# Two attention layers over 128 graphs: own orders for the first and last iterations, VectorE's loop written out, and the values of a layer's four graphs issued together

## The reference

```python
# layer 0
q, k, v = x@Wq+bq, x@Wk+bk, x@Wv+bv
h = softmax(where(adj == 0, -inf, q@k.T / sqrt(32))) @ v      # per head
y = layernorm(h@Wo+bo + x) * gamma + beta
# layer 1, on y
n = layernorm(y)*ln1_g+ln1_b;  q, k, v = n@wq+bq, n@wk+bk, n@wv+bv
o = softmax(q@k.T / sqrt(32) + where(adj > 0, 0.1*adj*adj, -inf)) @ v
x1 = y + o@wo+bo
out = x1 + gelu((layernorm(x1)*ln2_g+ln2_b)@w1+b1)@w2+b2      # w1 is 256x1024
```

## Time and profile before

| | |
|---|---|
| median of 3 runs | 2095.86 us (2091.73 to 2095.98) |
| profiled execution, own time | 2092.55 us |
| its span, first to last instruction | 2090.8 us |
| PE busy | 2040.8 us, 98% |
| ACT, DVE, POOL busy | 1649.2, 1598.8, 1007.9 us |
| mean granted TensorE clock | 0.993 of full |

### The profile page before, as it was taken

One profiled execution on the slowest core, in us unless ns is written; L12 is line 12 of the kernel. 1 busy time (PEld: TensorE's weight loads), 2 busy tenths in 40 slices (PEclk: granted clock), 3 DMA queues, 4 the chain that ended last, 5 costly groups with the idle time before them and its releaser, 6 DMA issues.

```text
span 2090.8 us, 59938 instructions
## 1 busy us (share of the span) xinstructions
PE 2040.8 (98%) x20032; PEld 1828.9 (87%) x20032; DVE 1598.8 (76%) x6911; ACT 1649.2 (79%) x5512; POOL 1007.9 (48%) x780
## 2 busy tenths in 40 slices
PE   6899999999999999999999999999999999999997
PEld 5689989889998889998889988889998889998886
DVE  5887877787877788777778777778777778777863
ACT  4688788878788878788888888887878887878863
POOL 3555445545445545445445445445455455455431
PEclk9999999999999999999999999999999999999999
DMA  4111100111100111100111100111100111101000
GB/s 139 32 32 42 42 27 16 40 40 40 40 18 22 40 40 40 40 11 29 40 40 40 40 10 30 40 40 40 40 10 30 40 40 40 37 13 31 27 11 21
DMA packets 80768, 72.80 MB, mean 35 GB/s; under 512 B 3009, under 2 KB 72257, under 8 KB 80705
## 3 DMA queue, kind: packets, MB, share of 16 engines
q1 hardware_dynamic: 80704, 71.98, 10.9%
HBM read 55.20 MB, written 16.78 MB: 34 GB/s over the span
## 4 chain that ended last, share of the span: by engine, by line
PE 94%; DVE 3%; ACT 2%; POOL 1%; issue 1%; DMA 0%; SPq 0%; ACTq 0%; DVEq 0%
PE ps L422 67%; PE ps L404 11%; PE ps L392 6%; PE ps L415 6%; PE ps L433 3%; ACT pm L539 1%; DVE pm L706 0%; DVE stats L780 0%; ACT hh L596 0%; DVE xy L795 0%; POOL y L890 0%; POOL y L895 0%; DMA pm<-in_wv 0%; ACT ps L597 0%; DVE actl L749 0%
## 5 line engine op out<-in xcount | busy, mean ns | idle before, releaser
L844 POOL TENSOR_TENSOR pm<-pm,rinv 128x512 f32<-128x512 f32 x512 | 520.8, 1041 | 604.8 <-DVE rinv L722 604.4
L539 ACT ACTIVATE pm<-pm,nmax 128x128 f32<-128x128 f32 x2048 | 792.7, 393 | 8.5 <-DVE nmax L706 8.1
L706 DVE CUSTOM_DVE_ANT_0 pm<-ps,m 128x128 f32<-128x128 f32 x2048 | 455.5, 285 | 38.5 <-PE ps L392 34.3
L539 ACT ACTIVATION_READ_ACCUMULATOR pm<-pm,nmax 128x1 f32 x2048 | 394.7, 193 | 0.0
L422 PE MATMUL ps<-w2h,hh 128*128 128x256 f32 x1024 | 295.6, 289 | 5.2 <-DVE hl L802 5.2
L404 PE MATMUL ps<-ident,pm 128*128 128x128 f32 x2048 | 290.7, 277 | 2.7 <-POOL pm L844 1.4
L422 PE MATMUL ps<-w2l,hh 128*128 128x256 f32 x1024 | 290.4, 284 | 0.0
L422 PE MATMUL ps<-w2h,hl 128*128 128x256 f32 x1024 | 290.4, 284 | 0.0
L863 POOL TENSOR_TENSOR rstd<-veps,power 128x4 f32<-128x4 f32 x96 | 97.3, 1014 | 370.4 <-DVE veps L788 370.3
L404 PEld LDWEIGHTS ps<-ident,pm 128*128 128x128 f32 x2048 | 230.7, 141 | 46.7 <-issue 19.5
L729 DVE COPY pt<-ps 128x512 f32<-128x512 f32 x256 | 176.0, 688 | 105.5 <-PE ps L404 105.4
(11 more groups left out here) (123 smaller groups left out, 5055.1 us busy)
## 6 DMA issues: line engine op xcount, KB each, us to landing
xTr<-in_xT SPq DMA_DIRECT2D x32, 512.0 KB, 4.6
xy<-in_x SPq DMA_DIRECT2D x32, 512.0 KB, 5.3
out<-x SPq DMA_DIRECT2D x32, 512.0 KB, 2.9
m<-in_adj SPq DMA_DIRECT2D x32, 256.0 KB, 2.8
a<-in_adj SPq DMA_DIRECT2D x32, 256.0 KB, 2.8
pt<-in_w SPq DMA_DIRECT2D x2, 512.0 KB, 8.8
pt<-in_w SPq DMA_DIRECT2D x1, 1024.0 KB, 12.0
r<-in_wo SPq DMA_DIRECT2D x2, 256.0 KB, 6.1
```

The source lines that it names most:

```text
L539: last = nc.scalar.activation(pm[:, g, h, :], pm[:, g, h, :], ACT.Exp, bias=nmax[:, g, h:h + 1], scale=-1.0, accum_out=rsum[:, g, h:h + 1])
L706: last = nc.vector.tensor_tensor_reduce(out=pm[:, g, h, :], in0=src[:, at:at + N], in1=m[:, g, :], scale=1.0, scalar=3e38, op0=ALU.add, op ...
L844: tt(pm[:, g, hs, :], pm[:, g, hs, :], rinv[:, g, hs].rearrange("p (h a) -> p h a", a=1).to_broadcast([P, HC, N]), ALU.mult).then_inc(norm ...
```

## The change

1. `JOBS` gets another order and other banks, and QKV0's jobs 0 and 1 now belong to the iteration itself instead of the one before. The loops still run over i = 5 to 30.
2. In the loop, and in head and tail, both halves of `values` of a layer stand directly behind each other on TensorE.
3. The first and last iterations have orders of their own, `HEAD` and `TAIL`, and each engine has a `head()` and `tail()` written for them.
4. VectorE's 26 loop iterations are written out; the other engines keep `Fori`.
5. ACT's DMA queue loads the first `xT` and the columns. Each of wq, wk and wv has its own semaphore, and DVE splits wq while the others arrive.
6. `BIAS` 0 moves in between the two halves of the first scores, `BIAS` 1 in behind the first graph's flips.
7. The last batch is stored in two halves.

```diff
-FIRST, LAST = -1, NB - 1 + 3
-FIRST_FULL, LAST_FULL = 5, NB - 1 + FIRST
+FIRST_FULL, LAST_FULL = 5, NB - 2
...
+        def iterate(eng, head, body, tail, written_out=False):
+            head()
+            if written_out:
+                for i in range(FIRST_FULL, LAST_FULL + 1):
+                    body(i)
+            else:
+                with eng.Fori(FIRST_FULL, LAST_FULL + 1) as i:
+                    body(i)
+            tail()
...
 # SP: store
+                if isinstance(b, int) and b == NB - 1:
+                    for j in (0, 1):
+                        taken(sp, b, "MLP2", j)
+                        gs = slice(2 * j, 2 * j + 2)
+                        sp.dma_start(o_b[b, :, gs, :], x1[:, gs, :]).then_inc(out_stored, 16)
...
 # TensorE
+            def head():
+                qkv(X, 0, 0); qkv(X, 0, 1); qkv(X, 0, 2); qkv(X, 0, 3); scores(X, 0, 0); shift_products(0)
+                scores(X, 0, 1); qkv(X, 0, 4); qkv(X, 0, 5); flip(X, 0, 0, 0); flip(X, 0, 0, 1); second_products(0)
+                flip(X, 0, 1, 0); flip(X, 0, 1, 1); flip(X, 0, 2, 0); flip(X, 0, 2, 1); flip(X, 0, 3, 0)
+                flip(X, 0, 3, 1); values(X, 0, 0); values(X, 0, 1); out_proj(X, 0, 0); out_proj(X, 0, 1); qkv(X, 1, 0)
...
             def body(i):
-                qkv(X, i, 2); mlp_down(i - 3, 0); mlp_down(i - 3, 1); qkv(X, i, 3); flip(Y, i - 2, 1, 0)
-                flip(Y, i - 2, 1, 1); mlp_down(i - 3, 2); scores(X, i, 0); values(Y, i - 2, 0); flip(Y, i - 2, 2, 0)
-                flip(Y, i - 2, 2, 1); mlp_down(i - 3, 3); qkv(X, i, 4); flip(Y, i - 2, 3, 0); flip(Y, i - 2, 3, 1)
-                qkv(X, i, 5); flip_rows("T1", i - 1, 0); flip_rows("T1", i - 1, 1); values(Y, i - 2, 1)
-                scores(X, i, 1); flip(X, i, 0, 0); out_proj(Y, i - 2, 0); qkv(Y, i - 1, 0); out_proj(Y, i - 2, 1)
-                qkv(Y, i - 1, 1); flip(X, i, 0, 1); qkv(Y, i - 1, 2); shift_products(i); qkv(Y, i - 1, 3)
-                flip(X, i, 1, 0); qkv(Y, i - 1, 4); qkv(Y, i - 1, 5); flip(X, i, 1, 1); flip_rows("T2", i - 2, 0)
-                flip_rows("T2", i - 2, 1); scores(Y, i - 1, 0); values(X, i, 0); flip(X, i, 2, 0); flip(X, i, 2, 1)
-                mlp_up(i - 2, 0); mlp_up(i - 2, 1); flip(X, i, 3, 0); flip(X, i, 3, 1); mlp_up(i - 2, 2)
-                out_proj(X, i, 0); mlp_up(i - 2, 3); mlp_up(i - 2, 4); mlp_up(i - 2, 5); values(X, i, 1)
-                flip(Y, i - 1, 0, 0); mlp_up(i - 2, 6); mlp_up(i - 2, 7); out_proj(X, i, 1); scores(Y, i - 1, 1)
-                second_products(i); flip(Y, i - 1, 0, 1); qkv(X, i + 1, 0); qkv(X, i + 1, 1)
+                qkv(X, i, 0); qkv(X, i, 1); qkv(X, i, 2); qkv(X, i, 3); mlp_down(i - 3, 0); mlp_down(i - 3, 1)
+                flip(Y, i - 2, 0, 1); scores(X, i, 0); flip(Y, i - 2, 1, 0); flip(Y, i - 2, 1, 1); mlp_down(i - 3, 2)
+                mlp_down(i - 3, 3); flip(Y, i - 2, 2, 0); flip(Y, i - 2, 2, 1); qkv(X, i, 4); flip(Y, i - 2, 3, 0)
+                flip(Y, i - 2, 3, 1); qkv(X, i, 5); flip_rows("T1", i - 1, 0)
+                values(Y, i - 2, 0); values(Y, i - 2, 1); scores(X, i, 1); flip_rows("T1", i - 1, 1)
+                out_proj(Y, i - 2, 0); flip(X, i, 0, 0); out_proj(Y, i - 2, 1); flip(X, i, 0, 1); qkv(Y, i - 1, 0)
+                flip(X, i, 1, 0); qkv(Y, i - 1, 1); qkv(Y, i - 1, 2); qkv(Y, i - 1, 3); qkv(Y, i - 1, 4)
+                qkv(Y, i - 1, 5); flip_rows("T2", i - 2, 0); flip_rows("T2", i - 2, 1); scores(Y, i - 1, 0)
+                flip(X, i, 1, 1); flip(X, i, 2, 0); mlp_up(i - 2, 0); mlp_up(i - 2, 1); flip(X, i, 2, 1)
+                mlp_up(i - 2, 2); flip(X, i, 3, 0); flip(X, i, 3, 1); mlp_up(i - 2, 3)
+                values(X, i, 0); values(X, i, 1); mlp_up(i - 2, 4); mlp_up(i - 2, 5); mlp_up(i - 2, 6)
+                out_proj(X, i, 0); mlp_up(i - 2, 7); out_proj(X, i, 1); scores(Y, i - 1, 1); flip(Y, i - 1, 0, 0)
+
+            def tail():
...
+                flip_rows("T1", 31, 1); out_proj(Y, 30, 0); out_proj(Y, 30, 1); qkv(Y, 31, 0); qkv(Y, 31, 1)
+                qkv(Y, 31, 2); qkv(Y, 31, 3); qkv(Y, 31, 4); qkv(Y, 31, 5); flip_rows("T2", 30, 0); scores(Y, 31, 0)
+                flip_rows("T2", 30, 1); mlp_up(30, 0); mlp_up(30, 1); mlp_up(30, 2); mlp_up(30, 3); mlp_up(30, 4)
+                mlp_up(30, 5); mlp_up(30, 6); mlp_up(30, 7); scores(Y, 31, 1); flip(Y, 31, 0, 0); mlp_down(30, 0)
+                mlp_down(30, 1); mlp_down(30, 2); flip(Y, 31, 0, 1); mlp_down(30, 3); flip(Y, 31, 1, 0)
+                flip(Y, 31, 1, 1); flip(Y, 31, 2, 0); flip(Y, 31, 2, 1); flip(Y, 31, 3, 0); flip(Y, 31, 3, 1)
+                values(Y, 31, 0); values(Y, 31, 1); out_proj(Y, 31, 0); out_proj(Y, 31, 1); flip_rows("T2", 31, 0)
...
 # ScalarE
+            def load_first():
+                sc.dma_start(xTr[:, :, :], xT_v[:, :, 0:T]).then_inc(xT_loaded, 16)
+                sc.dma_start(par[:, :], w["columns"]).then_inc(cols_loaded, 16)
...
 # VectorE
+            def split_part(n, by):
+                dve.wait_ge(part_loaded[n], 16)
...
+            def head():
+                split_q()
+                split_kv(0); x_lo(0, 0); x_lo(0, 1); mask0(0); mask_scores(X, 0, 0, 0); mask_scores(X, 0, 0, 1)
...
             def body(i):
...
+                residual("WO1", i - 2, 1); norm_stats(2, i - 2); copy_pt(X, i, 0); mask_scores(X, i, 3, 1)
+                norm_rows(2, i - 2); mask1(i - 1); recip(X, i, 2); v_out(Y, i - 1, 0); recip(X, i, 3)
+                lo("T2", i - 2, 0); lo("T2", i - 2, 1); mask_scores(Y, i - 1, 0, 0); mask_scores(Y, i - 1, 0, 1)
...
+            iterate(dve, head, body, tail, written_out=True)
```

More of the change, by code:

```diff
@@ L36, with count_uses, uses_before @@
 JOBS = [
[12 rows of a table removed]
[11 rows of a table added]
 ]
+ONCE = {("BIAS", 0): 7, ("BIAS", 1): 7}
 BANKS = 8
-FIRST, LAST = -1, NB - 1 + 3
-FIRST_FULL, LAST_FULL = 5, NB - 1 + FIRST
+FIRST_FULL, LAST_FULL = 5, NB - 2
+HEAD = [
[37 rows of a table added]
+]
+TAIL = [
[19 rows of a table added]
+]
 def exists(b):
     return 0 <= b < NB if isinstance(b, int) else True
-POS = {(name, n): at for at, (name, n, _, _) in enumerate(JOBS)}
-BEHIND = [job[2] for job in JOBS]
-BANK = [job[3] for job in JOBS]
 def first(b):
     return isinstance(b, int) and b == 0
[L70 to L83, removed]
+BANK = {**{(name, n): bank for name, n, _, bank in JOBS}, **ONCE}
+BEHIND = {(name, n): behind for name, n, behind, _ in JOBS}
+PER_LOOP = [sum(bank == k for _, _, _, bank in JOBS) for k in range(BANKS)]
+def count_uses():
+    steady = [(name, n, i - behind) for i in range(FIRST_FULL, LAST_FULL + 1) for name, n, behind, _ in JOBS]
+    uses, before = [0] * BANKS, {}
+    for at, (name, n, b) in enumerate(HEAD + steady + TAIL):
+        before[name, n, b] = uses[BANK[name, n]], at
+        uses[BANK[name, n]] += 1
+    return before
+BEFORE = count_uses()
+def uses_before(b, name, n):
+    if isinstance(b, int):
+        return BEFORE[name, n, b][0]
+    behind, every = BEHIND[name, n], PER_LOOP[BANK[name, n]]
+    return (b + behind) * every + (BEFORE[name, n, FIRST_FULL - behind][0] - FIRST_FULL * every)
 def place(h):
@@ L211, in filled @@
         def filled(eng, b, name, n):
-            pos = POS[name, n]
-            eng.wait_ge(job_full[BANK[pos]], uses_before(b + BEHIND[pos], pos) + 1)
-            return ps[BANK[pos]]
+            eng.wait_ge(job_full[BANK[name, n]], uses_before(b, name, n) + 1)
+            return ps[BANK[name, n]]
         def taken(eng, b, name, n):
-            pos = POS[name, n]
-            eng.wait_ge(job_free[BANK[pos]], uses_before(b + BEHIND[pos], pos) + 1)
+            eng.wait_ge(job_free[BANK[name, n]], uses_before(b, name, n) + 1)
         def taken_all(eng, b, outs, jobs):
             last = {}
-            for job in sorted(jobs, key=lambda job: (BEHIND[POS[job]], POS[job])):
-                last[BANK[POS[job]]] = job
+            when = b if isinstance(b, int) else FIRST_FULL - max(BEHIND.values())
+            for job in sorted(jobs, key=lambda job: BEFORE[(*job, when)][1]):
+                last[BANK[job]] = job
             for out in outs:
-                last.pop(BANK[POS[out]], None)
+                last.pop(BANK[out], None)
             for name, n in last.values():
@@ L260, in program @@
         BQ, BK, BV, LG, LB = 0, 2, 4, 6, 7
+        xT_v = xT.rearrange("(c p) n -> p c n", p=P)
         block = ctx.enter_context(nc.Block())
@@ L269, in _, with load_xT @@
             o_b = w["out"].rearrange("(b g) t f -> b t g f", g=G)
-            xT_v = xT.rearrange("(c p) n -> p c n", p=P)
             def row(name):
                 return w[name].rearrange("(a n) -> a n", a=1).to_broadcast([P, D])
-            def load_xT(b, ahead=False):
-                if exists(b) and (ahead or not first(b)):
+            def load_xT(b):
+                if exists(b) and not first(b):
                     need(sp, act_hi[0], C * b)
@@ L508, in _ @@
+            iterate(pe, head, body, tail)
         @block.scalar
@@ L614, in _ @@
```

(2 more changed lines are left out.)

361 lines of the change are left out of this document (289 added, 72 removed), and 79 rows, old and new, of tables (HEAD, JOBS, TAIL).

## The result

The kernel after takes 2085.8 us (median of 7 runs), the kernel before 2094.99 us in 7 runs beside it: a ratio of 0.9957, interval 0.9946 to 0.9969. (One execution of the 7 took 2517 us at a clock of 0.749 and stands outside the comparison.) So it is faster, by 0.43% where 1.0% was forecast; 2085.8 us lies inside the range, at its upper part.

A forecast was written before the change was run, and what follows sets the result against it. TensorE, busy for 98% of the span, was taken as the bound. Savings of 9.4 + 0.7 + 8.6 + 1.6 = 20.3 us from 2092.55 us gave 2072.2, taken as 2073 us; range 2064 to 2090 us.

The forecast's parts named there:

- the head: First batches before the loop: start, BIAS 1 and an earlier output projection together save 8.6 us; later waits stay unchanged.
- the tail: Last batches after the loop: wait before MLP2 shortened, other waits added, half store sooner; 1.6 us less in all.
- values joined, loop and six batches: Joined values halves save 0.36 us an iteration: 9.4 us over 26 loop iterations, 0.7 us at the ends.
- start: Kernel start: earlier xT and splitting wq and wk while wv arrives save 2.0 us, bounds 0 and 2.5.
- BIAS 1: Head: moved behind the first flips, it is hidden by batch 0's softmax; saves 5.1 us, bounds 3 and 5.1.
- first projection of batch 1 starts at: Head: batch 1's first projection should start near 42.5 us.
- behind it, to T2(0): Head, from batch 1's first projection to transpose 2 of batch 0: waits left as they were, bounds 4 us either way.
- the head gives its gain back: Rival: low clock and norm chain leave only loop and start gains, about 2080 us; chance 0.10 alone.
- T2 to MLP: Loop, narrowest wait, transpose 2 to MLP1 0: cover 2.92 us against a 2.70 us chain, 0.22 us left; cost taken 0.
- `mask1` delayed nothing: Slower rival, loop: `mask1` delays the low parts before MLP1 0, 1.6 us an iteration, 2114 us; chance 0.07.
- the exit: Loop: time lost after a group of values before work of another form, 0.18 us; two saved an iteration.
- VectorE written out: Loop: less register work, more instruction fetch on an engine with slack; taken as 0.

The follow-up runs named there:

- bias_back: Kernel after with BIAS 1 again behind batch 0's output projection, ahead of batch 1's first projection: 2089.94 us, ratio 0.9976 to the kernel before.
- rows_first: v_bank7 with VectorE's `norm_rows` ahead of batch 1's two reciprocals: 2079.52 us, ratio 0.9927 to the kernel before.
- v_bank7: Kernel after with three banks exchanged: QKV0 4 on bank 7, V1 0 on 3, V1 1 on 7: 2080.7 us, ratio 0.9942 to the kernel before.
- ends2: Kernel after with rows_alone's edits, x_lo_first, 40 warming transposes, batch 30's transpose 2 undivided and its second low part before masks: 2074.93 us, ratio 0.9912.
- warm: Kernel after with 55 identity transposes into an idle bank ahead of the first projection: 2083.29 us, ratio 0.9954 to the kernel before.
- rows_alone: rows_first with GpSimd's two `lo_w2` moved behind batch 1's `normalise`: 2078.45 us, ratio 0.9922 to the kernel before.
- v_apart: Kernel after with one other job between the two halves of values, in the loop alone: 2104.31 us, ratio 1.0044 to the kernel before.
- root_first: v_bank7 with both of GpSimd's roots ahead of the two `lo_w2`: 2083.71 us, ratio 0.9952 to the kernel before.
- x_lo_first: Kernel after with x's two low parts ahead of the split of wv on VectorE: 2083.34 us, ratio 0.9949 to the kernel before.

## Why the prediction was right or wrong

The step that failed is the head, as the prediction put it: "For the two batches after it I leave the waits as they were". They grew by more than the head had gained in front of them. Between the profiled executions 6.8 us were gained of 20.3 forecast; of the missing 13.5 us the head has 8.7, the loop 3.7 and the tail 1.1. That the time still lies inside the stated range says nothing for the mechanism. Term by term:

| term | forecast | measured | by |
|---|---|---|---|
| values joined, loop and six batches | 10.1 us | 6.4 us | T2(0) to T2 of batch 29 |
| start | 2.0 us | 0.5 us | first matmul at 11.09 instead of 11.57 us |
| BIAS 1 | 5.1 us | 3.3 us at batch 1's projection, 5.2 us at T2(0) | bias_back |
| first projection of batch 1 starts at | 42.5 us | 46.21 us | timeline |
| behind it, to T2(0) | 0 us | 5.0 us lost | 84.6 against 79.6 us |
| tail | 1.6 us | 0.5 us | T2 of batch 29 to the end |

**The head.** Two edits put the 5 us right: in rows_first, from batch 1's projection to T2(0), it is 125.44 - 46.06 = 79.4 us, against 79.6 us before. v's bank had 3.0 us of it (81.6 us in v_bank7), `norm_rows` beside GpSimd 2.2 us. The waits took more than the 5 us: from batch 1's first scores to T2(0) it is 77.2 us against 70.6 us, but the projection itself gave back 1.6 us, since it ran at full clock and not at 0.50 as in the kernel before (7.4 us to the scores instead of 9.0). I checked the narrow banks of the loop and not those of the head, where nothing else stands between S0 and v.

The rival "the head gives its gain back" had 0.10; of its two causes the norm chain was right, though its 2080 us, too, lie 6 us below what was measured. The clock did fall behind BIAS 1, but on batch 0's flips, and again on v of batch 1; it was back at 1.00 for batch 1's projection. With all edits the head gives 130.71 - 121.50 = 9.2 us (ends2), but that includes the warming transposes, which the forecast's 8.6 us did not count and which alone gave 3.5 us (warm). Without them no run reached 8.6 us.

**BIAS 1** was misread in one point: in the kernel before not everything was ready for batch 1 at 45.97 us. VectorE made the low parts of its x only from 48.24 us on:

```profile
48.24 1.28 DVE L749 TENSOR_TENSOR actl<-xTr,acth 128x512 fp32r<-128x512 f32 x2
```

The first of the two ends near 48.9 us, so by estimate the old order of VectorE would have let only some 2 us be gained. The new order makes them earlier, which the prediction didn't count on.

**The start** was sized 1.5 us too high. I placed only the split of v's third behind wv and forgot that wq itself would land later, and that x's low parts stand behind that split and three small operations. Of the 3.7 us by which batch 1 came later than forecast, this is 1.5. Another 0.9 is the first projection, 9.3 us against 8.4: 13 of its matmuls stand 0.42 us or more from the next instead of 8, and 0.23 us is the distance after that. 0.43 us is also the distance where the granted clock is 0.50, but here the profile's row says 1.00. Other runs of the same order had 8.2 to 9.2 us, so this is no effect of the change. The last 1.3 us lie between batch 0's scores and batch 1's projection. Two things stand there, and no run takes either away alone: a window (columns as in the earlier trace rows), then rows of VectorE, GpSimd and TensorE.

```profile
34.00:40.00 6.00, 6.00 (x29) 5.80 (x29) 4.16 (x9) 4.45 (x16) 5.54 (x5) 0.50 0.00 0
```
```profile
39.15 2.32 DVE L961 TENSOR_TENSOR actl<-xTr,acth 128x512 fp32r<-128x512 f32 x1
...
38.56 2.36 POOL L1189 TENSOR_TENSOR xy<-xy,bo 128x1024 f32<-128x1024 f32 x1
...
42.12 1.08 PE L493 MATMUL ps<-pt,v 128*32 128x128 f32 x32 [0.62 <-DVE pt L941]
```

Behind BIAS 1's single-column matmuls the flips ran at 0.50. And a low part of x, 0.64 us at the start of the kernel, takes 2.32 us beside GpSimd; the copy for which the second half of the values waits stands behind it.

**The loop** was right in mechanism: no wait arose (T2 to MLP kept its cover, `mask1` delayed nothing), and only the exits went. The size was off: the exit is 0.14 us and not 0.18, because I took the pitch of 0.026 us from modelled ends. From one and two halves, 64p + e = 1.884 and 32p + e = 1.011, it is 0.0273 us. Two exits are 0.28 us; the period fell by 0.25. Over 26 iterations that is 6.5 us instead of 9.4.

**VectorE written out** was costed at nothing, and was nothing.

**The tail.** The 2.02 us wait before MLP down is gone, but up to T2 of batch 30 only 1.0 us is gained. Five other waits, 2.3 us in all, stand there now, against one of 0.3 us before; the longest is this:

```profile
1993.25 0.36 PE L500 MATMUL ps<-wo1h,oth 128*128 128x256 f32 x1 [1.07 <-DVE actl L955]
```

Behind it, the wait before MLP up is 1.7 us longer (2.25 against 0.56 us; 1.4 us were forecast), and a clock of 0.87 in MLP up costs 1.6 us (12.7 us against 11.1 us in v_bank7). In v_bank7, where that clock is 1.00, T2 of batch 29 to the end takes 131.4 us, 2.5 us less than before. So with the same waits and the clock at 1.00 the tail gives more than the 1.6 us; what took them back in the kernel after is the clock. What lets the clock fall there in some kernels (after, warm) and not in others (v_bank7, rows_alone) with the same order wasn't found out.

The 2.4 us by which the profiled execution before lies under its median go with the clock too. Among the executions of the kernel before beside v_apart, six with a mean clock of 0.993 took 2091.3 to 2092.7 us, and eight with 0.989 to 0.991 took 2095.1 to 2097.9 us; the profiled one had 0.993. (Beside other kernels, some with 0.993 took up to 2094.6 us.) What sets the clock is open.

## What to carry to other kernels

When hidden work is taken off a chain, lay out what follows it too, with each job's bank: the gain is only there if the next wait doesn't grow by as much. An order that costs nothing in a full loop can cost microseconds in the first iterations, where no other job stands between a bank's last reader and its next writer. Where a VectorE instruction is waited for, look at what GpSimd runs beside it before moving anything of GpSimd's earlier.

## What the runs showed of the hardware

**VectorE is held by GpSimd.** `norm_rows` (SBUF to SBUF, float32, four instructions) took 1.38 us with GpSimd idle (rows_first, rows_alone), 3.49 us beside GpSimd's `normalise` of 1.07 us each (v_bank7), and 6.19 us beside two `lo_w2` of 2.34 us and then two `normalise` (root_first). Each instruction that met a GpSimd operation took about as long as that operation, or as the rest of it (1.12, and 2.42 and 1.75 us), instead of 0.40 us. The Trainium skill (SBUF — State Buffer, Who interferes with whom) says that the two engines share a pair of ports, which one of them holds for a whole instruction; by that rule, the trace agrees.

**A wait can cost more than its length.** Behind 3.80 us of waiting, TensorE's clock was at 0.50 (1.2 GHz) for the 5.4 us of v, which cost 2.5 us beyond the wait. Behind the same wait v took 4.4 us in x_lo_first and 4.8 us in bias_back, so this cost changes from kernel to kernel by 1 us, and differences of T2(0) of that size prove nothing alone.
